# Moving the guard of the squared norms from GpSimd to VectorE in a six-layer attention stack

## The reference

```python
q = l2norm(q) * qs                 # t / max(norm(t), 1e-12)
k = l2norm(k) * ksc
q = q * cos * scale + rotate_half(q) * sin * scale
k = k * cos * inv + rotate_half(k) * sin * inv
out = local_attention(q, k, v)     # softmax over at most 64 keys
x = out.reshape(b, n, INNER) @ Wo + x
x = ffn_layer(shift_tokens(x), ...) + x
```

## Time and profile before

| | us |
|---|---|
| median of 3 runs | 2491.36 (2491.31 to 2496.53) |
| profiled execution, its time | 2495.51 |
| its span | 2493.7 |
| VectorE busy in it | 1873.9 |
| GpSimd busy in it | 1493.1 |
| TensorE busy in it | 2083.0 |

### The profile page before, as it was taken

The page is one execution under the profiler, slowest core; times in us unless marked ns, Lnnn a source line. Parts: engine busy times, 40 slices in busy tenths (PEclk is TensorE's granted clock), DMA queues, the critical chain, the costliest instruction groups (busy, mean ns, idle before and its releaser), DMA issues. The chain is left out here.

```text
span 2493.7 us, 81632 instructions
## 1 busy us (share of the span) xinstructions
PE 2083.0 (84%) x33532; PEld 1459.8 (59%) x33532; DVE 1873.9 (75%) x3984; ACT 1536.9 (62%) x5170; POOL 1493.1 (60%) x1253
## 2 busy tenths in 40 slices
PE   5649999899898999988999989999999983765287
PEld 2337667476574775757757567576675741433165
DVE  4569789498795887968969679597896946775744
ACT  2238778487684886857858578586785841551022
POOL 1149779398693896948959579596794930211000
PEclk8669999999999999998999999999999996876599
DMA  2011111111011110101101011011110100001000
GB/s 92 0 39 38 32 30 51 32 42 35 26 52 33 40 39 21 51 25 49 38 22 51 26 51 38 20 51 31 46 39 15 39 13 11 1 0 52 1 0 17
DMA packets 86570, 80.52 MB, mean 32 GB/s; under 512 B 15040, under 2 KB 82624, under 8 KB 85568
## 3 DMA queue, kind: packets, MB, share of 16 engines
q1 hardware_dynamic: 86208, 75.37, 10.5%
HBM read 25.51 MB, written 1.05 MB: 11 GB/s over the span
## 5 line engine op out<-in xcount | busy, mean ns | idle before, releaser
L992 POOL TENSOR_TENSOR RN<-N2G,minus_half 128x8 f32<-128x8 f32 x384 | 738.0, 1922 | 32.0
L985 POOL TENSOR_TENSOR RR<-R 128x512 f32<-128x512 f32 x384 | 485.6, 1265 | 204.3 <-DVE R L934 204.3
L831 ACT ACTIVATE PB<-PS,NMX 128x64 f32<-128x64 f32 x1536 | 460.7, 312 | 69.3 <-DVE NMX L951 69.1
L710 PE MATMUL PS<-WQ,XS 128*128 128x256 f32 x1536 | 440.0, 409 | 13.4 <-SPq L541 13.1
L653 PE MATMUL PS<-ident,QK 128*128 128x128 f32 x1536 | 255.3, 289 | 102.4 <-DVE QK L921 71.7
L831 ACT ACTIVATION_READ_ACCUMULATOR PB<-PS,NMX 128x1 f32 x1536 | 312.0, 203 | 0.0
L710 PEld LDWEIGHTS PS<-WQ,XS 128*128 128x128 f32 x1536 | 263.8, 191 | 70.2 <-SPq L541 13.3
L810 ACT ACTIVATE QKT<-PS 128x512 f32<-128x512 f32 x384 | 229.4, 597 | 97.8 <-PE PS L653 91.6
L266 POOL TENSOR_TENSOR rstd<-ve,minus_half 128x4 f32<-128x4 f32 x40 | 40.5, 1012 | 400.4 <-DVE ve L236 347.1
L941 DVE TENSOR_REDUCE N<-SQ 128x8 f32<-128x512 f32 x384 | 257.1, 670 | 10.8 <-ACT SQ L805 10.7
L921 DVE TENSOR_TENSOR QK<-RR,RN 128x512 f32<-128x512 f32 x384 | 260.6, 679 | 1.7 <-POOL RR L985 1.6
(11 more groups left out here) (209 smaller groups left out, 3550.9 us busy)
## 6 DMA issues: line engine op xcount, KB each, us to landing
VS<-XB SPq DMA_DIRECT2D x384, 96.0 KB, 2.1
VS<-XB SPq DMA_DIRECT2D x288, 32.0 KB, 2.1
WQ<-in_wqkv SPq DMA_DIRECT2D x40, 192.0 KB, 2.4
WO<-in_wo SPq DMA_DIRECT2D x6, 512.0 KB, 3.7
BIG<-in_wgu SPq DMA_DIRECT2D x1, 2048.0 KB, 7.8
W<-in_w SPq DMA_DIRECT2D x6, 341.0 KB, 4.0
WQ<-in_wqkv SPq DMA_DIRECT2D x1, 1536.0 KB, 11.7
QKS<-in_qks SPq DMA_DIRECT2D x6, 256.0 KB, 3.3
```

Source lines behind the costliest of these rows:

```text
L710: mm = nc.tensor.matmul(PQ[:, (g + 3) % 2, j * 256:(j + 1) * 256], XSb[b][:, t0:t0 + P], WQ[:, pair * 384:pair * 384 + 256], start=True, s ...
L831: ex = nc.scalar.activation(PB[:, g % 2, u, :], SC[:, h, DH * t:DH * t + DH], ACT.Exp, bias=NMX[:, u:u + 1], accum_out=PSUMS[:, g % 2, u:u ...
L985: nc.gpsimd.tensor_tensor(RR[:, :, :], R1[:, :, :], R2[:, :, :], ALU.add)\
L992: nc.gpsimd.tensor_tensor(RN[:, g % 2, :], N2G[:, g % 2, :], minus_half[:, :], ALU.pow)
```

## The change

The guard is no longer a GpSimd instruction. VectorE does it as an instruction of its own in the same step, behind the reciprocal of the softmax sums (L948) and ahead of the row maxima (L951), where it waits for VectorE's own sum of squares. GpSimd's power waits for `n2g_in` as before, which VectorE now signals. The flow `n2_in` is settled by VectorE instead of GpSimd. Tiles, buffers, and the number of instructions over all engines stay the same.

```diff
--- before.py
+++ after.py
@@ -946,6 +946,10 @@
                             if g + 2 >= TOTAL:
                                 dve.wait_ge(p_in.sem, p_in.take())
                             nc.vector.reciprocal(RO[:, k, :], PSUMS[:, k, :]).then_inc(ro_in.sem, 1)
+                        if there(g + 2):
+                            dve.wait_ge(n2_in.sem, n2_in.take())
+                            nc.vector.tensor_scalar(N2G[:, g % 2, :], N2[:, g % 2, :], 1e-24, None, ALU.max)\
+                                .then_inc(n2g_in.sem, 1)
                         if there(g):
                             dve.wait_ge(sc_in.sem, sc_in.take())
                             nc.vector.tensor_reduce(
@@ -963,7 +967,7 @@
 
                     for g in range(-3, TOTAL + 3):
                         step(g)
-                    for f in (rr_in, table_in, sq_in, p_in, sc_in, ro_in, layer_dve, wo_in, x_in_dve, to_tokens,
+                    for f in (rr_in, table_in, sq_in, n2_in, p_in, sc_in, ro_in, layer_dve, wo_in, x_in_dve, to_tokens,
                               stats_in, aggr_in, rstd_in, gelu_in, up_in, xo_dve):
                         f.settle(dve)
 
@@ -985,9 +989,6 @@
                             nc.gpsimd.tensor_tensor(RR[:, :, :], R1[:, :, :], R2[:, :, :], ALU.add)\
                                 .then_inc(rr_in.sem, 1)
                         if there(g + 2):
-                            pool.wait_ge(n2_in.sem, n2_in.take())
-                            nc.gpsimd.tensor_scalar(N2G[:, g % 2, :], N2[:, g % 2, :], 1e-24, None, ALU.max)\
-                                .then_inc(n2g_in.sem, 1)
                             pool.wait_ge(n2g_in.sem, n2g_in.take())
                             nc.gpsimd.tensor_tensor(RN[:, g % 2, :], N2G[:, g % 2, :], minus_half[:, :],
                                                     ALU.pow)
@@ -996,7 +997,7 @@
 
                     for g in range(-3, TOTAL + 3):
                         step(g)
-                    for f in (rot_in, n2_in, n2g_in, var_in, qks_in):
+                    for f in (rot_in, n2g_in, var_in, qks_in):
                         f.settle(pool)
 
             with nc.Fori(0, B) as b:
```

## The result

The changed kernel takes 2599.68 us (median of 6 runs, 2596.64 to 2609.83) against 2492.44 us for the kernel before beside it. The ratio is 1.0434, 95% interval 1.0414 to 1.0453: slower by 107 us, where 2604 us was forecast and 113 us was the sum. The profiled execution has a span of 2597.1 us, 103.4 more than before.

A forecast was written before the change was run, and what follows sets the result against it. It took the layer-stack step, 3.643 us with VectorE and GpSimd blocking each other, as the bound. 346 steps lengthened to 3.96 us (110 us) plus 3 us, on the median 2491.4, gave 2604 us; range 2560 to 2680.

The forecast's parts named there:

- the sum: Whole kernel: 346 steps x (3.96 - 3.643) = 110 us, plus 3 us for seven more steps, together 113 us slower.
- The loop of one step: Layer stack: L985, guard, L951, L957, L921, L933, L934, back to L985, forecast at 3.96 us a step.
- addition: GpSimd's L985 in each layer-stack step, taken as 1.27 us of the loop.
- start of the maxima: VectorE's L951 behind the guard, forecast to start 0.05 us before L985's end.
- maxima to probabilities: VectorE's L951 to L957, start to start, forecast at 0.34 us.
- probabilities to L921: VectorE's L957 to L921, forecast at 0.34 us, as L957 would now meet no L985.
- L921 to L934's end: VectorE from L921's start to L934's end, taken as 1.88 us, with 0.18 us more to the next L985.
- The blocked guard: Guard on VectorE held by L985, about 0.8 us long, ending 0.02 us behind it; 2604 us, chance 0.85.
- third rival: GpSimd's power (L992) holds the shared lane for 1.67 us, blocking L957: step 5.31 us, +577 us, 3068 us; chance 0.02.
- seven further steps: Steps outside the twelve undisturbed stretches of the layer stack, 7 x 0.42 = 3 us slower.
- first rival: Guard on VectorE not blocked beside L985, under 0.2 us: step 3.54 us, -37 us, 2454 us; chance 0.10.
- SP's transfers gain time: At the forecast step of 3.96 us, SP's transfers would have more time; no size given.

The follow-up runs named there:

- halved addition: Changed kernel with GpSimd's addition issued as two instructions of 256 elements each instead of one of 512: 2522.66 us, ratio 1.0096 to the kernel before.
- two-input guard: Changed kernel with the guard as a tensor_tensor, maximum of the sums and a tile of 1e-24, both in SBUF: 2605.14 us, ratio 1.0425.
- tensor_reduce: Changed kernel with the guard, in the same place, as a maximum over pairs of the sum and 1e-24: 2473.48 us, ratio 0.9904; again 2472.19 us, 0.9895.
- late wait: SP's wait for the next layer's weights moved two steps later: on the tensor_reduce kernel 2466.74 us, 0.9879; on the kernel before 2496.52 us, 0.9999.

## Why the prediction was right

**The loop of one step.** Forecast 3.96 us, measured 3.94. By its terms: addition 1.27 (1.27), start of the maxima 0.06 us ahead of its end (0.05), maxima to probabilities 0.33 (0.34), probabilities to L921 0.34 (0.34), L921 to L934's end 1.88 (1.88), then 0.17 (0.18). Each term came from a row of the kernel before in which that piece stood undisturbed, but for the end of the guard, which was worked out from the 0.28 us of the larger operations.

**The blocked guard.** The open question was whether eight elements stand still as 256 do. They do: forecast an end 0.02 us behind the addition, measured 0.03, and 323 us of new busy time on VectorE where some 300 were expected. The halved addition and the two-input guard show the cause by moving and by keeping the stall; the tensor_reduce takes it away. The Trainium skill says of the shared pair (SBUF — State Buffer, "Who interferes with whom") that whichever side issues first has it for the whole instruction and the other blocks. That holds for the addition: the guard waited until its end and took 0.85 us. It does not hold to the letter for the power: L961 ran in 0.41 us from 448.03, inside a power that ran from 447.86 to 449.51. That was the third rival (3068 us), and it did not come.

**The sum.** 113 us forecast, 107 measured between medians, 103 between the spans. The 0.02 us too much in the step makes 7 us over 346 steps: 102.6 us in the trace where 110 were forecast. The seven further steps gave 2.8 us (forecast 3). For the rest, of which the prediction counted 24 and the trace has 30, nothing was forecast, and 4.0 us less came. That is two things against each other, neither foreseen: the intervals with a feed-forward block take 1.9 us more, and the odd steps near them 5.9 us less, because seven steps of 4.3 us and two of 5.7 and 5.8 us there are now ordinary ones of 3.9 to 4.0 us.

**The first rival** (guard slips through, 3.54 us) described exactly the step of the kernels without a blocked guard, but its time was too low: 0.985 of the kernel before against 0.9904 and 0.9917 measured. It left out that shorter steps leave SP less time for its transfers; the late wait shows that path, though not its size in the kernel's time, and with it the ratio is still 0.9879. Part of the remaining gap is TensorE's clock in the feed-forward blocks, told at the end. The sentence "SP's transfers gain time" held only for the slower case.

## What to carry to other kernels

Before an instruction is moved from GpSimd to VectorE, look at which GpSimd instruction runs at the moment it will be issued, and whether its form is one that stands still beside it; its size says nothing. Put an instruction that is held behind what others wait for, or write it in a form with one SBUF input that is not held (here a tensor_reduce over pairs). And read a full engine with care: GpSimd had no idle time before, but part of its busy time was itself the other engine's hold.

## What the runs showed of the hardware

- A tensor_scalar and a tensor_tensor of 8 elements took 0.85 us beside a GpSimd addition of 512, and a tensor_reduce of 16 took 0.17 us in the same place.
- The order decides more than the hold: a blocked guard ahead of the probabilities (3.62 us a step) beat an unblocked one of 0.16 us behind them (3.71 us), because GpSimd's power then started behind QK and took 2.02 us instead of 1.65.
- The power let a two-input VectorE operation that started 0.17 us behind it run inside it at 0.41 us; one of 256 elements that met the addition ended 0.27 us or more behind the addition's end. Why they differ was not tried.
- A power issued while a two-input VectorE operation ran ended 1.49 to 1.53 us behind that operation's end, in every trace; otherwise it took 1.64 to 1.67 us.
- In the kernel before and in the changed one, intervals with a feed-forward block come in two lengths, 40.6 to 40.7 and 42.3 to 42.4 us (the last of a trace 40.2), at changing places. The longer ones have a lower granted clock of TensorE. Two of the kernel before, as start and end, length, busy us of PE, PEld, VectorE, ScalarE and GpSimd, and behind them the granted clock as a share of 2.4 GHz:

```profile
606.15:648.47 42.32, 38.30 (x196) 18.10 (x196) 17.72 (x49) 13.36 (x31) 16.36 (x9) 0.96 0.04 12
761.96:802.66 40.70, 36.59 (x196) 17.43 (x196) 17.71 (x48) 13.43 (x31) 7.42 (x7) 1.00 0.03 7
```

- In the first, the two groups of matmuls behind an idle stretch of 0.87 us run at the lower level, 1.2 GHz, for some 3.5 us; the same matmuls behind the same idle stretch in the second keep 2.4 GHz:

```profile
633.65 2.07 PE L616 MATMUL PS<-XN,W 128*128 128x512 f32 x2 [0.87 <-ACT XN L769]
...
789.45 1.12 PE L616 MATMUL PS<-XN,W 128*128 128x512 f32 x2 [0.87 <-ACT XN L769]
```

- The stretch at 1.2 GHz costs some 1.7 us. It is in two of the eleven intervals of the kernel before, in three of the changed one, in five and three of the two runs of the tensor_reduce kernel and in four of that with the late wait. What puts it into one block and not into the next stays open.
- The tensor_reduce kernel and the one without a guard have intervals of 42.1 to 42.7 us at the full clock, which hold a wait for SP's weights of 1.1 to 1.8 us, and of 43.8 to 44.5 us, which hold such a wait and a stretch at the lower clock together.
